# Token routing of a mixture-of-experts kernel: pair weights stored behind the normalized rows, ranks summed by TensorE, lane masks on two engines

## Chip, cores, metric

One core of a Trainium2 chip runs the whole program. The metric is the device time of one execution in microseconds (us), the median over runs.

## The reference, cut to what matters

Eight sequences of 512 tokens (4096 tokens, 256 numbers each) pass through cross attention to a context of 1601 rows, causal self attention, and a mixture of experts. Only the last part is touched by the change:

```python
logits = xf @ w_router                       # 4096 tokens x 8 experts
probs = softmax(logits)
topw, topi = top_k(probs, 2)                 # the two best experts of a token
topw = topw / sum(topw)
combine = sum(one_hot(topi, 8) * topw[..., None])
g, u = silu(xf @ wg[x]), xf @ wu[x]          # hidden size 704
out = sum over experts x of combine[:, x] * ((g * u) @ wd[x])
y = h + out
```

## The kernel before

The kernel is a row of stages with a barrier after each (`Prog.clear`): `prepare_weights`, `project_inputs`, `attention` (cross), `project_self`, `attention` (self), `finish_self`, `route`, `experts`. In a stage each engine has its own written-out program and the engines meet at semaphores: an instruction waits for a count, and a finished one raises one. PE is TensorE, DVE VectorE, ACT ScalarE, POOL GpSimd, SP the queue that issues plain transfers.

**`finish_self`** makes for each batch of 512 tokens the normalized rows, stores them to `hn_rows` in DRAM (a table of 4096 rows of 256 numbers; `store_normed`, L1432), and leaves the router's logits in SBUF. Token number t*128+p lies in partition p, column t (T = 32 columns).

**`route`** sorts the 8192 (token, expert) pairs by expert into tiles of 128 slots. There are 72 tiles, since every expert is padded to a whole tile.
- DVE alone takes the softmax, the two best experts (`first`, `second`, each a 0/1 mask of 128x32x8) and the two pair weights (L1646 to L1680). ACT takes the exponential.
- PE multiplies the choice mask by a triangular matrix (rank of a token within its column, `ps_rank`, L1786) and by ones (count of each column, `ps_total`, L1788). DVE turns the counts of the columns into running sums by five doubling steps (L1684 to L1692).
- DVE counts the tiles of each expert, finds the expert of each tile (`tile_cmp`, `tile_f`, `tile_expert`, L1646 to L1706), then the slot of each pair, and splits it into a tile number and a lane (L1708 to L1723).
- The mask loop has 16 chunks, each of 4 columns of pairs. DVE compares tile numbers to 0..71 (`in_tile`, L1729, 128x4x72) and lanes to 0..127 (`at_lane`, L1733, 128x4x128). POOL multiplies `in_tile` by the token numbers and again by the pair weights (`at_tile`, L1758, two instructions of 128x288). PE sums 4 products of `at_lane` and `at_tile` into `ps_slots` (L1795, 144 columns). The profile lists two instructions for each such f32 product. All masks have two buffers, so chunk n waits for `slots_done` of chunk n-2.
- DVE takes from `ps_slots` three tables in SBUF: token, target row and weight of every slot (L1738 to L1746).
- SP meanwhile loads the down-projection weights of all experts (`wd_sb`, L1772, L1774).

**`experts`** goes over 71 tiles of 128 slots. POOL gathers the rows of a tile from `hn_rows` with an indirect DMA (`gather`, L1888), up to two tiles ahead, and adds the result into `sums` in DRAM with another (`add_up`, L1901). PE turns the rows (L1930), multiplies by gate and up weights (L1941), turns the hidden values (L1949) and multiplies by the down weights (L1959). ACT takes SiLU and scales the result by the slots' weights (`result`, L2009). DVE multiplies gate and up (L2040), copies the turned hidden values (L2046, L2047), and copies one column of the weight table for each tile (`take_weight`, L2034). POOL's own order is: gather of tile k+4, `add_up` of tile k, gather of tile k+5, and so on.

## Time and profile before

| what | value |
|---|---|
| median of 3 runs | 2792.38 us (2789.43 to 2793.11) |
| the profiled execution | 2793.06 us, its span 2791.3 us |
| stages `route` and `experts` by the timeline | about 2117 to 2176 us and from 2177 us on |
| busy share of the span | PE 92%, DVE 64%, ACT 52%, POOL 26% |

The profile lists every instruction of one execution with its engine, line, start and duration. Where an instruction stood idle before it ran, a bracket tells how long and who ended the wait. PEld is the loading of a matmul's stationary operand. PEclk is the granted clock of TensorE as a share of 2.4 GHz, so 0.50 is 1.2 GHz. The chain of work that ended last runs in its last part over the tiles of `experts`.

### The profile page before, as it was taken

The page shows a single profiled execution, that of the slowest core. Times are in us where ns is not written, and L with a number is a line of the kernel's source. Part 1 is how long each engine was busy: PE and PEld are TensorE (multiplying, and loading weights), DVE is VectorE, ACT ScalarE, POOL GpSimd, SP SyncE. Part 2 cuts the span into 40 slices and gives each one's busy share as a digit, 9 for nine tenths or more (in the row PEclk, how much of TensorE's full clock was granted, in tenths as well). Part 3 has the DMA queues.
Part 4 walks back from the last instruction along what each step waited for, and adds up shares of the span by engine and source line. Part 5 has one row for each costly group of instructions (what it writes and reads, how often), then busy time and mean ns, then how long its engine had stood idle before and what let it go on. Part 6 is the DMA issues. An engine that isn't in the chain of part 4 may idle for free. (4 is left out here: it accounts for less than half of the span.)

```text
span 2791.3 us, 47210 instructions
## 1 busy us (share of the span) xinstructions
PE 2575.7 (92%) x14174; PEld 1302.7 (47%) x14175; DVE 1786.7 (64%) x3812; ACT 1453.8 (52%) x2957; POOL 737.0 (26%) x1327
## 2 busy tenths in 40 slices
PE   6999899999999999999997877999884899999996
PEld 4665233333333333333332543444364677777775
DVE  4665888888888888888882766777445222222221
ACT  2333277777777777777775654777521122222221
POOL 4444100000000000000002664666444333333332
PEclk9999699999999999999998998999886999999998
DMA  6777845455555544555513867898574121212123
GB/s 202 224 228 201 117 54 62 57 63 67 67 67 67 62 61 58 61 62 67 67 20 103 244 200 141 162 162 161 135 226 134 25 32 32 32 32 32 32 32 79
DMA packets 494486, 274.38 MB, mean 98 GB/s; under 512 B 309296, under 2 KB 462784, under 8 KB 494112
## 3 DMA queue, kind: packets, MB, share of 16 engines
q1 hardware_dynamic: 472224, 239.77, 44.9%
q0 software_dynamic: 16192, 30.16, 5.7%
q10 hardware_dynamic: 5888, 2.24, 0.4%
q8 instruction: 88, 1.44, 0.3%
q14 instruction: 94, 0.77, 0.1%
HBM read 172.15 MB, written 103.31 MB: 99 GB/s over the span
## 5 line engine op out<-in xcount | busy, mean ns | idle before, releaser
L879 DVE TENSOR_REDUCE att_cross_neg_max<-att_cross_ps_s 128x1 f32<-128x401 f32 x2048 | 1027.2, 567 | 150.8 <-PE att_cross_ps_s L798 148.4
L973 ACT ACTIVATE att_cross_probs<-att_cross_ps_st 128x512 f32<-128x512 f32 (+1 forms) x1664 | 879.4, 601 | 288.9 <-PE att_cross_ps_st L817 276.8
L798 PE MATMUL att_cross_ps_s<-att_cross_k_pack,att_cross_q_pack 96*128 96x401 bf16 x2048 | 655.8, 343 | 11.9 <-DVEq L865 11.4
L817 PE MATMUL att_cross_ps_st<-att_cross_q_pack,att_cross_k_pack 99*128 99x512 bf16 (+1 forms) x1664 | 630.4, 382 | 6.5 <-ACT att_cross_probs L973 5.0
L832 PE MATMUL att_cross_ps_o<-att_cross_probs,att_cross_v_tiles 128*32 128x512 f32 (+1 forms) x3328 | 443.0, 604 | 0.1
L798 PEld LDWEIGHTS att_cross_ps_s<-att_cross_k_pack,att_cross_q_pack 96*128 96x128 bf16 x2048 | 201.1, 98 | 372.2 <-DVE att_cross_neg_max L879 242.9
L921 POOL CAST att_cross_neg_max_parts<-att_cross_neg_max_merged 128x16 bf16<-128x16 f32 x32 | 6.3, 196 | 1134.8 <-DVE att_cross_neg_max_merged L872 1134.8
L817 PEld LDWEIGHTS att_cross_ps_st<-att_cross_q_pack,att_cross_k_pack 99*128 99x128 bf16 (+1 forms) x1664 | 163.8, 99 | 303.5 <-ACT att_cross_probs L973 191.9
L879 DVE TENSOR_REDUCE att_self_neg_max<-att_self_ps_s 128x1 f32<-128x128 f32 (+3 forms) x512 | 221.5, 484 | 96.8 <-PE att_self_ps_s L801 94.7
L973 ACT ACTIVATE att_self_probs<-att_self_ps_st 128x256 f32<-128x256 f32 (+3 forms) x512 | 201.0, 437 | 95.2 <-PE att_self_ps_st L817 86.0
L2046 DVE COPY moe_hiddenT<-moe_ps_h 128x256 f32<-128x256 f32 x142 | 60.2, 424 | 296.9 <-PE moe_ps_h L1949 296.9
L2003 ACT ACTIVATE moe_silu<-moe_ps_g 128x352 f32<-128x352 f32 x142 | 65.7, 463 | 301.3 <-PE moe_ps_u L1941 301.3
L1959 PE MATMUL moe_ps_y<-top_wd_sb,moe_hiddenT 128*128 (+1 forms) x852 | 196.0, 379 | 1.1 <-DVE moe_hiddenT L2047 1.1
L1941 PE MATMUL moe_ps_g<-top_wg_sb,moe_rowsT 128*128 x568 | 192.8, 462 | 0.0
L1941 PE MATMUL moe_ps_u<-top_wu_sb,moe_rowsT 128*128 x568 | 192.3, 461 | 0.0
L798 PE MATMUL att_self_ps_s<-att_self_k_pack,att_self_q_pack 96*128 96x128 bf16 (+3 forms) x512 | 155.3, 313 | 36.1 <-DMA att_self_q_pack<-q_parts 20.2
L1901 POOL DMA_INDIRECT sums<-moe_y,moe_target x71 | 113.4, 1597 | 281.1 <-ACT moe_y L2009 136.2
L1959 PEld LDWEIGHTS moe_ps_y<-top_wd_sb,moe_hiddenT 128*128 128x128 f32 (+1 forms) x852 | 161.6, 190 | 35.1 <-issue 1.4
L934 POOL TENSOR_SCALAR_AFFINE_SELECT att_self_probs<-att_self_probs 128x128 f32<-128x128 f32 x512 | 143.8, 292 | 115.9 <-ACT att_self_probs L973 105.5
L2040 DVE TENSOR_TENSOR moe_hidden<-moe_ps_u,moe_silu 128x352 f32<-128x352 f32 x142 | 73.4, 517 | 133.2 <-ACT moe_silu L2003 131.6
L817 PE MATMUL att_self_ps_st<-att_self_q_pack,att_self_k_pack 99*128 99x256 bf16 (+3 forms) x512 | 151.8, 309 | 2.4 <-ACT att_self_probs L973 1.5
L1941 PEld LDWEIGHTS moe_ps_u<-top_wu_sb,moe_rowsT 128*128 128x128 f32 x568 | 108.5, 191 | 60.7 <-issue 1.0
(220 smaller groups left out, 2886.2 us busy)
## 6 DMA issues: line engine op xcount, KB each, us to landing
att_cross_k_pack<-k_parts SPq DMA_DIRECT2D x192, 200.1 KB, 7.3
k_parts<-in_part SPq DMA_DIRECT2D x72, 256.0 KB, 3.3
in_rows<-in_ctx_dram SPq DMA_DIRECT2D x24, 512.0 KB, 4.5
v_rows<-in_v_biased SPq DMA_DIRECT2D x24, 512.0 KB, 2.9
att_cross_q_pack<-q_parts SPq DMA_DIRECT2D x192, 64.0 KB, 7.8
att_cross_v_tiles<-v_rows SPq DMA_DIRECT2D x128, 96.0 KB
att_self_k_pack<-k_parts SPq DMA_DIRECT2D x192, 64.0 KB, 3.7
att_self_q_pack<-q_parts SPq DMA_DIRECT2D x192, 64.0 KB, 3.7
```

The lines of the kernel that those rows point to most:

```text
L798: mm = nc.tensor.matmul(ps_s[bank][:, 0:w], qp[v.buf][0:SROWS, j, q * P:(q + 1) * P], kp[v.buf][0:SROWS, j, s:s + w], start=True, stop=not ...
L817: mm = nc.tensor.matmul(ps_st[bank_of_step[s]][0:rows, q0:SEQ], kp[u.buf][0:MROWS, j, t * P:t * P + rows], qp[u.buf][0:MROWS, j, q0:SEQ], ...
L832: nc.tensor.matmul(ps_o[j * VW:(j + 1) * VW, q0:SEQ], va[packs.vbuf(u)][0:rows, t, j, :], pr[0:rows, (u.odd * STEPS + t * GH + j) % RING, ...
L879: nc.vector.tensor_reduce(nmax[v.odd][:, j * QT + q, i:i + 1], ps_s[bank][:, 0:w], AX.X, ALU.max, negate=True).then_inc(s_read, 1)
L934: nc.gpsimd.affine_select(out=diagonal, in_=diagonal, pattern=[[1, P]], base=0, channel_multiplier=-1, compare_op=ALU.is_ge, fill=0.0).the ...
L973: nc.scalar.activation(pr[0:rows, (u.odd * STEPS + s) % RING, q0:SEQ], ps_st[bank_of_step[s]][0:rows, q0:SEQ], ACT.Exp).then_inc(exp_done, 1)
L1901: pool.indirect_dma_start(out=sums, in_=y[t.par][:, :], in_offset=None, compute_op=ALU.add, out_offset=bass.IndirectOffsetOnAxis(ap=target ...
L1941: last = nc.tensor.matmul(ps[half][:, 0:HHALF], xT[t.par][:, i, :], wt[:, bass.ds(at, HHALF)], start=(i == 0), stop=(i == KC - 1))
L1959: last = nc.tensor.matmul(ps_y[:, :], hT[half][0:CW[c], c, :], wd[0:CW[c], bass.ds(at, DIM)], start=(half == 0 and c == 0), stop=(half == ...
L2003: nc.scalar.activation(sil[half][:, :], ps_g[half][:, 0:HHALF], ACT.Silu).then_inc(sil_ready, 1)
L2040: nc.vector.tensor_tensor(h[half][:, :], ps_u[half][:, 0:HHALF], sil[half][:, :], ALU.mult)\
L2046: nc.vector.tensor_copy(hT[half][:, 0:CH - 1, :], ps_h[half][:, 0:CH - 1, :])
```

## The change

The weight of a pair is no longer carried through the mask loop. POOL makes a table of 4096 x 8 weights (`dense`, zero for experts not chosen), and ACT's queue stores it into eight more columns of `hn_rows`, whose rows grow from 256 to 264 numbers. The gather brings these with the row. `take_weight` multiplies the tile's eight gathered columns by a one-hot row of the tile's expert (`tile_of_expert`) and adds them up. It now stands first in DVE's step, and POOL's gather waits for it, since it frees the row buffer.

The ranks are summed by PE: the triangular product, then 32 products with ones, each added to all later columns of `ps_rank`, and column T holds the totals. The doubling steps and two additions on DVE fall away.

In the mask loop POOL's `at_tile` is gone. The lane mask is made one column at a time, as a compare with the lane and a multiply by the token number in one instruction of 128x128. In even chunks DVE makes two of them and POOL two, in odd chunks DVE one and POOL three. PE's products have 72 columns instead of 144. The expert of each tile is found after the loop instead of before it.

```diff
@@ finish_self, store_normed
-                    sp.dma_start(batch_rows(hn_rows, b), hn[b % 2][:, :, :]).then_inc(hn_sent[b % 2], 16)
+                    sp.dma_start(batch_rows(hn_rows[:, 0:DIM], b), hn[b % 2][:, :, :]).then_inc(hn_sent[b % 2], 16)
@@ route, new helpers
+        def pool_share(n):
+            return range(2 - n % 2, C)
+        def token_at_lane(engine, n, c):
+            k, t = n * C // T, n * C % T + c
+            return engine.tensor_scalar(at_lane[n % 2][:, c, :], keep["iota_lane"][:, :], lane_of[:, k, t:t + 1],
+                                        keep["token"][:, t:t + 1], ALU.is_equal, ALU.mult)
@@ route, vector
+                nc.vector.memset(chosen[:, T, :], 0.0)
+                nc.vector.memset(past[:, :, 0:1], 1.0)
...
                 dve.wait_ge(ranks_done, 1)
-                nc.vector.tensor_copy(run[0][:, :, :], ps_total[:, :, :])
-                dve.drain()
-                src, step = 0, 1
-                while step < T:
-                    a, b = run[src], run[1 - src]
-                    nc.vector.tensor_copy(b[:, 0:step, :], a[:, 0:step, :])
-                    tt(b[:, step:T, :], a[:, step:T, :], a[:, 0:T - step, :], ALU.add)
-                    src, step = 1 - src, step * 2
-                total = run[src]
...
-                tt(tile_cmp[:, 0:TILES, :], over_e(keep["iota_tile"][:, 0:TILES], TILES),
-                   end[:, :].unsqueeze(1).broadcast_to([P, TILES, E]), ALU.is_ge)
-                reduce(tile_f[:, 0:TILES], tile_cmp[:, 0:TILES, :], ALU.add)
-                nc.vector.tensor_scalar(expert[:, 0:TILES], tile_f[:, 0:TILES], E - 1.0, None, ALU.min)
-                tt(place[:, :, :], total[:, :, :], ps_total[:, :, :], ALU.subtract)
-                tt(place[:, :, :], place[:, :, :], ps_rank[:, :, :], ALU.add)
...
                 for n in range(CHUNKS):
                     if n >= 2:
                         dve.wait_ge(slots_done, n - 1)
-                        dve.wait_ge(tile_ready, n - 1)
                     (in_tile as before)
-                    nc.vector.tensor_tensor(at_lane[n % 2][:, :, :], ...ALU.is_equal).then_inc(lane_ready, 1)
+                    for c in range(pool_share(n)[0]):
+                        last = token_at_lane(nc.vector, n, c)
+                    last.then_inc(lane_ready, 1)
+                tt(past[:, :, 1:E + 1], over_e(keep["iota_tile"][:, 0:TILES], TILES),
+                   end[:, :].unsqueeze(1).broadcast_to([P, TILES, E]), ALU.is_ge)
+                nc.vector.tensor_tensor(of_expert[:, :, :], past[:, :, 0:E], past[:, :, 1:E + 1], ALU.subtract)
+                reduce(tile_f[:, :], past[:, :, 1:E + 1], ALU.add)
+                nc.vector.tensor_scalar(expert[:, 0:TILES], tile_f[:, :], E - 1.0, None, ALU.min)
                 dve.wait_ge(slots_done, CHUNKS)
-                nc.vector.tensor_copy(keep["slot_weight"][:, :], ps_slots[:, 1, :])
@@ route, gpsimd
+                pool.wait_ge(weights_ready, 2)
+                for k, pick in enumerate((first, second)):
+                    nc.gpsimd.tensor_tensor(dense[k][:, :, :], pick[:, :, :], over_e(weights[:, k, :]), ALU.mult)...
+                nc.gpsimd.tensor_tensor(dense[0][:, :, :], dense[0][:, :, :], dense[1][:, :, :], ALU.add)...
+                pool.wait_ge(lanes_ready, 1)
                 for n in range(CHUNKS):
                     if n >= 2:
                         pool.wait_ge(slots_done, n - 1)
-                    pool.wait_ge(in_tile_ready, n + 1)
-                    for a, values in enumerate((keep["token"][:, ts], weights[:, k, ts])):
-                        last = nc.gpsimd.tensor_tensor(at_tile[n % 2][:, :, a, :], in_tile[n % 2][:, :, :], ...)
-                    last.then_inc(tile_ready, 1)
+                    for c in pool_share(n):
+                        last = token_at_lane(nc.gpsimd, n, c)
+                    last.then_inc(pool_lane_ready, 1)
@@ route, sync and scalar
+                sp.wait_ge(dense_sent, 16)
+                act.wait_ge(dense_step, 3)
+                act.dma_start(hn_rows[:, DIM:DIM + E].rearrange("(t p) e -> p t e", p=P), dense[0][:, :, :])
@@ route, tensor
-                nc.tensor.matmul(ps_total..., ones[:, :], chosen...).then_inc(ranks_done, 1)
+                for t in range(T):
+                    last = nc.tensor.matmul(ps_rank[:, t + 1:T + 1, :], ones[:, :],
+                                            chosen[:, t, :].unsqueeze(1).broadcast_to([P, T - t, E]),
+                                            start=False, stop=(t == T - 1))
+                last.then_inc(ranks_done, 1)
...
-                        last = nc.tensor.matmul(ps_slots..., at_lane[n % 2][:, c, :], at_tile[n % 2][:, c, :, :]...)
+                        last = nc.tensor.matmul(ps_slots[:, :], at_lane[n % 2][:, c, :], in_tile[n % 2][:, c, :], ...)
@@ experts, gpsimd, gather
                     pool.wait_ge(turned, t.n + 1)
+                    pool.wait_ge(weight_ready, t.n + 1)
@@ experts, vector
+                dve.sem_inc(weight_ready, 2)
-                def take_weight(t):
-                    dve.wait_ge(y_ready, t.n)
-                    nc.vector.tensor_copy(weight[t.par][:, :], keep["slot_weight"][:, bass.ds(t.n, 1)])...
+                def take_weight(t, first=False):
+                    dve.wait_ge(rows_in[t.par], (t.turn + 1) * 16)
+                    if not first:
+                        dve.wait_ge(y_ready, t.n)
+                    nc.vector.tensor_tensor(weight_if[t.par][:, :], rows[t.par][:, DIM:DIM + EXPERTS],
+                                            keep["tile_of_expert"][:, bass.ds(t.n, 1), :]..., ALU.mult)
+                    dve.drain()
+                    nc.vector.tensor_reduce(weight[t.par][:, :], weight_if[t.par][:, :], AX.X, ALU.add)
                       .then_inc(weight_ready, 1)
@@ experts, vector, step
+                    take_weight(t)
                     turned_hidden(t.next(-1), 1)
-                    take_weight(t)
                     multiply(t, 0)
```

## Rows read from the trace of the kernel before

**Rows 1.** Windows: busy time, counts, granted clock, DMA share of two stretches.
```profile
2138.50:2174.70 36.20, 23.45 (x128) 20.44 (x128) 21.59 (x33) 0.00 (x0) 28.40 (x32) 0.83 0.08 23
...
2181.10:2791.30 610.20, 586.60 (x2556) 434.28 (x2556) 159.71 (x496) 127.14 (x285) 210.32 (x281) 0.98 0.21 37
```

**Rows 2.** Waits from 2117 to 2176 us: total, times, longest.
```profile
PE route_ps_slots L1795 <- POOL route_at_tile L1758: 24.4, 14, 14.3
```

**Rows 3.** Timeline of the ranks and places: start, duration, engine.
```profile
2126.21 0.39 PE L1786 MATMUL route_ps_rank<-route_chosen,top_keep_before_b 128*128 128x256 bf16 x1 [10.11 <-DVE route_chosen L1675]
...
2126.40 0.42 PE L1788 MATMUL route_ps_total<-route_chosen,route_ones 128*128 128x256 bf16 x1
...
2127.28 0.42 DVE L1684 COPY route_run<-route_ps_total 128x256 f32<-128x256 f32 x1
...
2130.49 0.43 DVE L1646 TENSOR_TENSOR route_compare<-route_run,top_keep_constants 128x264 f32<-128x264 f32 x1
...
2132.33 0.76 DVE L1646 TENSOR_TENSOR route_tile_cmp<-top_keep_constants,route_end 128x576 f32<-128x576 f32 x1
...
2134.11 0.41 DVE L1646 TENSOR_TENSOR route_place<-route_run,route_ps_total 128x256 f32<-128x256 f32 x1
```

**Rows 4.** Timeline of the mask loop, its start, one period, its end.
```profile
2138.58 0.46 DVE L1729 TENSOR_TENSOR route_in_tile<-top_keep_constants,route_tile_of 128x288 f32<-128x288 f32 x1
...
2141.15 4.18 PE L1795 MATMUL route_ps_slots<-route_at_tile,route_at_lane 128*128 128x144 f32 x16 [14.34 <-POOL route_at_tile L1758]
...
2154.40 1.22 PE L1795 MATMUL route_ps_slots<-route_at_tile,route_at_lane 128*128 128x144 f32 x8 [1.17 <-POOL route_at_tile L1758]
2155.29 0.66 POOL L1758 TENSOR_TENSOR route_at_tile<-route_in_tile,route_pair_weights 128x288 f32<-128x288 f32 x1
...
2156.18 0.68 DVE L1733 TENSOR_TENSOR route_at_lane<-top_keep_constants,route_lane_of 128x512 f32<-128x512 f32 x1
...
2157.72 1.15 DVE L1733 TENSOR_TENSOR route_at_lane<-top_keep_constants,route_lane_of 128x512 f32<-128x512 f32 x1
...
2158.48 1.22 PE L1795 MATMUL route_ps_slots<-route_at_tile,route_at_lane 128*128 128x144 f32 x8 [1.17 <-POOL route_at_tile L1758]
...
2174.70 0.23 DVE L1738 COPY top_slot_weight<-route_ps_slots 128x72 f32<-128x72 f32 x1 [3.59 <-PE route_ps_slots L1795]
```

**Rows 5.** Timeline of POOL in self attention, four one-input instructions.
```profile
1702.60 1.23 POOL L934 TENSOR_SCALAR_AFFINE_SELECT att_self_probs<-att_self_probs 128x128 f32<-128x128 f32 x4 [0.42 <-ACT att_self_probs L973]
```

**Rows 6.** One line's instructions: DVE with two per-partition scalars.
```profile
L411 DVE TENSOR_SCALAR in_x_normed<-in_rows,in_norm_mean_var,in_norm_std_inv x32: 399/402/2075, 44.7 to 267.5; 128x256 f32<-128x256 f32 x32
```

**Rows 7.** Timeline of PE near the start: 128-column transposes.
```profile
23.43 3.68 PE L362 MATMUL in_ps_t<-top_keep_constants,in_rows 128*128 128x128 f32 x16 [9.16 <-DMA in_rows<-in_ctx_dram]
```

**Rows 8.** Windows: PE busy at either granted clock.
```profile
2147.10:2151.10 4.00, 2.61 (x18) 2.24 (x18) 2.66 (x4) 0.00 (x0) 3.37 (x4) 0.98 0.00 0
...
2106.00:2110.00 4.00, 3.97 (x19) 3.97 (x20) 0.19 (x1) 0.00 (x0) 1.93 (x3) 0.50 0.28 93
```

**Rows 9.** The page's DMA queues: packets, MB, share of 16 engines.
```profile
q10 hardware_dynamic: 5888, 2.24, 0.4%
```

**Rows 10.** Timeline of one expert tile's step.
```profile
2207.77 0.47 ACT L2009 ACTIVATE moe_y<-moe_ps_y,moe_weight 128x256 f32<-128x256 f32 x1 [2.13 <-PE moe_ps_y L1959]
...
2207.90 0.38 PE L1930 MATMUL moe_ps_x<-top_keep_constants,moe_rows 128*128 128x128 f32 x2
...
2208.53 0.28 DVE L2047 COPY moe_hiddenT<-moe_ps_h 96x128 f32<-96x128 f32 x1
...
2209.14 1.59 POOL L1901 DMA_INDIRECT sums<-moe_y,moe_target  x1 [3.99 <-PE moe_ps_x L1930]
...
2211.71 1.02 POOL L1888 DMA_INDIRECT moe_rows<-hn_rows,moe_source  x1 [0.79 <-POOL moe_source L1884]
...
2216.11 0.38 PE L1930 MATMUL moe_ps_x<-top_keep_constants,moe_rows 128*128 128x128 f32 x2
```

**Rows 11.** DMA issues of the experts: count, us to landing.
```profile
moe_rows<-hn_rows,moe_source POOLq DMA_INDIRECT x65, 2.8
```

More of the change, by code:

```diff
@@ L1587, in route @@
     CHUNKS = 2 * T // C
-    logits, expert = keep["logits"], keep["tile_expert"]
+    logits, expert, of_expert = keep["logits"], keep["tile_expert"], keep["tile_of_expert"]
     with ExitStack() as stack:
@@ L1598, in route @@
         top = [p.sb(f"top{i}", [P, T]) for i in range(2)]
-        run = [p.sb(f"run{i}", [P, T, E]) for i in range(2)]
+        weights = p.sb("pair_weights", [P, 2, T])
+        dense = [p.sb(f"dense_weights{i}", [P, T, E]) for i in range(2)]
         place = p.sb("place", [P, T, E])
-        compare = p.sb("compare", [P, E, 64])
+        compare = p.sb("compare", [P, E, T + 1])
         used = p.sb("used_tiles", [P, E])
@@ L1674, in _ @@
                         dve.drain()
-                nc.vector.tensor_tensor(chosen[:, :, :], first[:, :, :], second[:, :, :], ALU.add)\
+                nc.vector.tensor_tensor(chosen[:, 0:T, :], first[:, :, :], second[:, :, :], ALU.add)\
                   .then_inc(chosen_ready, 1)
@@ L1810, in experts @@
         p = Prog(nc, stack, "moe_")
-        rows = [p.sb(f"rows{i}", [P, DIM]) for i in range(2)]
+        rows = [p.sb(f"rows{i}", [P, DIM + EXPERTS]) for i in range(2)]
         xT = [p.sb(f"rowsT{i}", [P, KC, P]) for i in range(2)]
@@ L1819, in experts @@
         weight = [p.sb(f"weight{i}", [P, 1]) for i in range(2)]
+        weight_if = [p.sb(f"weight_if{i}", [P, EXPERTS]) for i in range(2)]
         ps_g = [p.ps(f"ps_g{i}", [P, SEQ]) for i in range(2)]
@@ L2050, in first @@
                 def first(t):
[L2051 removed]
+                    take_weight(t, True)
                     multiply(t, 0)
```

90 lines of the change are left out of this document (45 added, 45 removed).

## The prediction

> **What bounds the kernel now.** I read four views in this order. First the windows by stage. The experts take 610 us, in which PE is busy 587 us at clock 0.98 [rows 1]: PE bounds that stage, and nothing that the change takes from DVE or POOL there can shorten it. The mask loop of the routing takes 36.1 us, and PE works only 23.5 of them, while POOL is busy 28.4 [rows 1]. Second the waits: PE stood 24.4 us in all for POOL's `at_tile` (14.3 of it before the first one) [rows 2]; in the loop POOL is what comes last, chunk after chunk. Third the timeline. Two chunks follow each other every 2158.48 - 2154.40 = 4.08 us [rows 4], 2.04 us a chunk, and the loop ends on PE at 2174.7. Ahead of the loop DVE alone is the chain: from the ranks (2127.28) to the first mask (2138.58) it never waits for another engine [rows 3, 4]. So all that DVE does between the ranks and the first mask, and the loop itself, is on the path that sets the end, since the experts can't start before the barrier. Fourth the step of one expert tile, for slack [rows 10].
>
> **Ahead of the ranks.** Two short fills are added and a drain leaves. A short one-input instruction takes 0.23 us alone [rows 4] (the copy at 2174.70), less in a row. I take +0.1 us.
>
> **The ranks.** Before, two products of 256 bf16 columns start 0.19 us apart [rows 3], the speed of 1.2 GHz, one column a cycle. The new sum has one product of 264 columns and 32 of 256, 248, ... 8 columns. Down to 128 columns these are 17 with 3264 columns together, 2.72 us at 1.2 GHz. The other 15 are shorter than the load of 128 stationary columns, 0.107 us at one column a cycle, 1.6 us. With the first (0.22) and 0.2 for the last one's way through, this is 4.75 us from 2126.3, so 2131.05, and DVE begins its compare at about 2131.15 instead of 2130.49: **+0.7 us**. The doubling steps (3.2 us, 2127.28 to 2130.49) are thus not won but traded for PE's work. If loads don't hide beside products, 17 x 0.107 = 1.8 us come on top. If the clock were high throughout, 2.3 less. While DVE waits, POOL makes `dense`: three two-input instructions of 256 elements. The row of 288 elements takes 0.66 us [rows 4], so 2 us from 2127.0, done before DVE moves again: nothing on the path.
>
> **From the ranks to the first mask.** `tile_cmp`, its reduction and the conversion leave this place: 2134.11 - 2132.33 = 1.78 us [rows 3]. The two additions of 256 elements take 0.41 us and a gap of 0.08 each [rows 3]: 0.98 us. One drain: 0.1. Sum **-2.86 us**. The other instructions keep their shapes, and some read PSUM in place of SBUF (the row of 2134.11 did too, at no higher price). The loop starts at 2138.58 + 0.7 - 2.86 = 2136.4.
>
> **The mask loop.** Three bounds for a chunk.
> - PE: 8 instructions. At 1.2 GHz 16 of them took 4.18 us with 144 columns [rows 4]. With 72 columns the load of 128 stationary f32 columns is longer than the product. The nearest row is 16 transposes of 128 columns in 3.68 us [rows 7], 0.22 each: 1.76 us a chunk, with a gap 1.8. At 2.4 GHz half: 0.9 (8 with 144 columns took 1.22 with their latency [rows 4]).
> - POOL: no row shows a compare-and-multiply on POOL. The nearest has one input and 128x128 elements: four in 1.23 us, 0.31 each [rows 5]. The upper bound is the two-input instruction of 288 elements, 0.66 [rows 4]. Five in two chunks: 1.55 to 3.3 us. I take 0.31 to 0.35, since the shape and the one input agree.
> - DVE: `in_tile` 0.46 [rows 4], and three lane masks in two chunks. With two per-partition scalars and 256 elements DVE took 0.402 us [rows 6]; 128 elements less at 1 ns each (0.68 for 512 against 0.46 for 288 [rows 4]) makes 0.27. Sum 0.92 + 0.81 = 1.73 us in two chunks.
>
> POOL and DVE hinder each other in this trace: the same `at_lane` takes 0.68 us, or 1.15 with POOL at work [rows 4], and the line of [rows 6] has a median of 402 ns and a largest of 2075 ns. So two chunks of masks take between 1.73 (side by side) and 3.28 us (one after the other), with hand-over 1.15 to 1.7 us a chunk. At the high clock a chunk is then 1.35 us, at the low one 1.8 and PE sets it.
>
> The Trainium skill, SBUF — State Buffer, section Who interferes with whom, speaks against a loop split over these two engines: an f32 `tensor_scalar` on DVE can use the pair of ports that GpSimd uses, and whoever is second is blocked entirely. By that rule the loop is 16 x 1.64 + 0.9 = 27.1 us. The trace's 0.68 and 1.15 us [rows 4] agree that one blocks the other, but only in part.
>
> Which clock? The loop starts at 0.50, and in the kernel before it rose about 6 us after PE's start [rows 4, 8] and was 0.83 in the mean of the loop [rows 1]; it stayed 0.50 in a stretch where PE was busy 3.97 of 4 us with products of 8 columns [rows 8]. No row has 72 columns. I take 6 chunks at 1.8 and 10 at 1.35, with 0.9 until the first chunk's masks and 0.1 to DVE: 25.3 us against 36.1: **-10.8 us**. All low gives 29.8 (-6.3), nearly all high and hand-over short 20.5 (-15.6).
>
> **After the loop.** The weight copy leaves: -0.15 us. The search for each tile's expert now stands here: two compares or subtractions of 576 elements, a reduction and a conversion, 1.78 + 0.7 = 2.5 us [rows 3], where 0.76 us, less its fixed part, stands for the added one. It starts when DVE has made its masks of chunk 15, while PE has nearly two chunks ahead (2.7 to 3.6 us, less 0.9 for the masks). About 0.5 us stick out: **+0.35 us** together. Without that cover it would be 2.5.
>
> **The store of the weights.** 4096 pieces of 32 B. The queue that carried small pieces so far has 5888 packets in 0.4% of 16 x 2791 us [rows 9], 30 ns each; 4096 at 30 to 45 ns over 16 engines are 8 to 12 us, from about 2130 to 2142, more beside the wd loads. The stage ends at about 2163, so cover is left unless a piece costs over 130 ns (33 us x 16 / 4096): 0. The normed rows' stores keep their pieces of 1 KB, now 1056 B apart: +0.2 us, bound 0 to 2.
>
> **The experts.** Let S be PE's turn of the next rows, 2207.90 [rows 10]. DVE is free at 2208.81 (S+0.9), the result two tiles back is ready at S+0.34, so `take_weight` is done at S+1.3 and fits before the next hidden copy (DVE is busy 160 of 610 us in this stage [rows 1]). The gather issued then frees one step later than now: index copy and gap 1.0, issue, landing 2.8 us after its start [rows 11], at S+5.2. PE wants these rows at its next turn, 2216.11 or S+8.2 [rows 10]: 3 us are left. `add_up` now stands behind the gather and starts at S+4.5 instead of S+1.24 (2209.14), and it has landed before the `result` that waits for its predecessor. Three instructions in place of one on DVE, 71 times, lie under PE. I take +0.3 us for the first tiles.
>
> **The sum.** +0.1 +0.7 -2.86 -10.8 +0.35 +0.2 +0.3 = -12.0 us against the profiled 2793.06, so 2781.0. The median lies 0.7 us under it: **2780.5 us**.
>
> **Rivals.**
> - *A, POOL's compare-and-multiply is dear.* At 0.66 us two chunks take 3.3 + 0.5 = 3.8 us, the loop 31.3, and the time is 2786.5. At 0.82 (4.6 us for two) nothing is left of the gain of the whole change. For it: no row of this operation, two scalars are read besides. Against: [rows 5]. Chance 0.12.
> - *B, the gather's new wait takes the place of the weight table.* If rows land later than S+8.2, every tile is longer by the lateness, 70 us for each us. This ends on the slower side, from 3 us more than counted on. For it: the gather moves one whole step, and POOL has two indirect transfers in line behind it. Against: the slack in [rows 10, 11]. At 1 us of lateness 2850. Chance 0.06.
> - *C, the scattered store ends last*, from 130 ns a piece; at 170 ns the stage ends 10 us later, which makes 2791: no change. Chance 0.05.
>
> The Trainium skill, DMA: Bandwidth & Descriptors, section Specifications, says that pieces under 512 B are read, modified and written, which would speak for C. No row here shows a 32 B store; [rows 9] show small pieces without such a price.
>
> - *D, ports serialize wholly*, as the rule above has it: 2782.3, within the forecast.
>
> **The numbers.** The forecast has 0.74 with D, A 0.12, B 0.06, C 0.05, and something unseen 0.03. About 0.2% (5.6 us) is what a measurement of this kernel can tell from no change. The forecast's cases reach from 2775 (high clock, short hand-over) to 2785.5 (clock low throughout, ranks unhidden). With A's upper row the range is 2774 to 2787. Faster 0.82 (forecast and part of A), same 0.10 (the dearer end of A, and C), slower 0.08.
>
> **What would show it.** Compare starts near 2131 and the first mask near 2136.5; 16 chunks from there to `slots_done` in 20 to 30 us; PE's wait names DVE and POOL less, and its clock in that window tells which case it is; POOL's 128x128 mask at about 0.3 us; experts at 8.21 us a tile, with PE busy throughout; `ps_x` waiting for `moe_rows` would be B, SP waiting long after the last slot would be C.

## Result, and the profile after

| | before | after |
|---|---|---|
| median, runs on the same chip | 2792.23 us (20 runs) | 2795.92 us (20 runs) |
| ratio, 95% interval | | 1.0013 [1.0007, 1.0019] |
| the profiled execution, its span | 2793.06, 2791.3 | 2794.20, 2792.5 |

The change makes the kernel a little slower, by 0.13%. The interval does not reach 1, but the size is below the 0.2% that the prediction took for the least it could tell apart. 12 us were forecast to be won, and the median lies above the forecast's range of 2774 to 2787.

The timelines of the two executions, cut at the same events, show where. "First fill" is DVE's memset of `ones` at the start of `route`; "first mask" is the first `in_tile`; the loop ends where DVE reads `ps_slots`.

| stretch | before | after | difference | forecast |
|---|---|---|---|---|
| first fill to `compare` | 13.38 | 13.08 | -0.30 | +0.8 |
| `compare` to first mask | 8.09 | 5.17 | -2.92 | -2.86 |
| mask loop | 36.12 | 42.26 | **+6.14** | **-10.8** |
| loop's end to first gather | 3.58 | 3.47 | -0.11 | +0.35 |
| first gather to first `ps_x` | 2.88 | 3.46 | +0.58 | 0 |
| first `ps_x` to the end | 610.14 | 610.47 | +0.33 | +0.3 |
| sum | 674.2 | 677.9 | +3.7 | -12.2 |

The sum of +3.7 us is close to what the medians show (2795.92 - 2792.23). The profiled spans differ by 1.2 only, because the stages ahead of `route` were 2.5 us shorter in this one execution; over the runs below the first fill comes between 2111.7 and 2121.1 us, whatever the edit. The forecast column lacks the +0.2 us of the normed rows' stores, which lie ahead of the first fill. One row is far off, the mask loop. Here is the timeline of the changed kernel (start, duration, engine, line, names; in brackets the idle time before and who ended it), which answers to [rows 3, 4]:

```profile
2123.69 0.40 PE L1793 MATMUL route_ps_rank<-route_chosen,top_keep_before_b 128*128 128x264 bf16 x1 [10.10 <-DVE route_chosen L1688]
...
2123.89 3.74 PE L1796 MATMUL route_ps_rank<-route_chosen,route_ones 128*128 128x256 bf16 x32
...
2126.66 0.45 ACTq L1787 DMA_DIRECT2D hn_rows<-route_dense_weights  x1
...
2127.67 0.43 DVE L1657 TENSOR_TENSOR route_compare<-route_ps_rank,top_keep_constants 128x264 f32<-128x264 f32 x1 [3.14 <-PE route_ps_rank L1796]
...
2132.84 0.49 DVE L1724 TENSOR_TENSOR route_in_tile<-top_keep_constants,route_tile_of 128x288 f32<-128x288 f32 x1
...
2135.13 1.96 PE L1805 MATMUL route_ps_slots<-route_in_tile,route_at_lane 128*128 128x72 f32 x8 [7.50 <-POOL route_at_lane L1650]
...
2147.66 3.66 PE L1805 MATMUL route_ps_slots<-route_in_tile,route_at_lane 128*128 128x72 f32 x16 [1.40 <-POOL route_at_lane L1650]
2149.65 0.46 DVE L1724 TENSOR_TENSOR route_in_tile<-top_keep_constants,route_tile_of 128x288 f32<-128x288 f32 x1 [2.38 <-PE route_ps_slots L1805]
2149.72 4.41 POOL L1650 TENSOR_SCALAR route_at_lane<-top_keep_constants,route_lane_of 128x128 f32<-128x128 f32 x5 [0.65 <-PE route_ps_slots L1805]
...
2152.72 3.66 PE L1805 MATMUL route_ps_slots<-route_in_tile,route_at_lane 128*128 128x72 f32 x16 [1.40 <-POOL route_at_lane L1650]
...
2170.53 0.84 DVE L1657 TENSOR_TENSOR route_past_expert<-top_keep_constants,route_end 128x576 f32<-128x576 f32 x1
...
2173.03 0.20 DVE L1735 TENSOR_SCALAR top_tile_expert<-route_tile_f 128x72 int32<-128x72 f32 x1
...
2173.11 1.96 PE L1805 MATMUL route_ps_slots<-route_in_tile,route_at_lane 128*128 128x72 f32 x8 [1.54 <-POOL route_at_lane L1650]
2175.10 0.23 DVE L1738 TENSOR_SCALAR route_token_f<-route_ps_slots 128x72 f32<-128x72 f32 x1 [1.87 <-PE route_ps_slots L1805]
```

The period of two chunks is 2152.72 - 2147.66 = 5.06 us, before it was 4.08 [rows 4]. Read one period as a circle. POOL starts at 2149.72 with three masks for an odd chunk, each of them a row of the timeline here:

```profile
2149.72 1.15 POOL L1650 TENSOR_SCALAR route_at_lane<-top_keep_constants,route_lane_of 128x128 f32<-128x128 f32 x1 [0.65 <-PE route_ps_slots L1805]
...
2150.86 0.79 POOL L1650 TENSOR_SCALAR route_at_lane<-top_keep_constants,route_lane_of 128x128 f32<-128x128 f32 x1
...
2151.63 0.94 POOL L1650 TENSOR_SCALAR route_at_lane<-top_keep_constants,route_lane_of 128x128 f32<-128x128 f32 x1
```

They end at 2152.57, 2.85 us after the start. PE waits for the third of them (1.40 us idle) and starts 0.15 later, at 2152.72. After another 2.06 us POOL begins again, at 2154.78: a chunk of PE's takes 1.96 when it stands alone (the row of 2173.11), and 0.10 go to the hand-over. 2.85 + 0.15 + 2.06 = 5.06. The two masks of the even chunk lie beside PE's work. So three things stand on this circle: POOL's own price of a mask (0.79), PE's chunk at the low clock, and 0.5 us by which the first and the third mask are longer than the second. The first starts 0.07 us behind DVE's `in_tile` (2149.65), the third while the next `in_tile` is under way; e5 below shows whose doing that is. The instructions of the masks' line (shortest, median and longest, ns):

```profile
L1650 POOL TENSOR_SCALAR route_at_lane<-top_keep_constants,route_lane_of x40: 789/799/1152, 2132.8 to 2172.0; 128x128 f32<-128x128 f32 x40
L1650 DVE TENSOR_SCALAR route_at_lane<-top_keep_constants,route_lane_of x24: 334/341/428, 2133.3 to 2170.3; 128x128 f32<-128x128 f32 x24
```

The waits from 2117 to 2176 us (total, times, longest), which answer to [rows 2]:

```profile
DVE route_in_tile L1724 <- PE route_ps_slots L1805: 24.3, 14, 2.7
PE route_ps_slots L1805 <- POOL route_at_lane L1650: 17.8, 9, 7.5
```

A mask costs POOL 799 ns in the median; DVE makes the same one in 341. Five take POOL 4.41 us, 0.88 each, of which 0.5 us in all are those longer ones. PE's wait for POOL has not gone: it was 24.4 us before with a first wait of 14.3 [rows 2], and is 17.8 now with a first one of 7.5, so some 10 us behind the first chunk in either kernel, and PE is slower meanwhile. The windows (busy time and count of PE, PEld, DVE, ACT and POOL, granted clock, DMA share, GB/s), which answer to [rows 1, 8]:

```profile
2132.84:2175.10 42.26, 29.63 (x128) 28.06 (x128) 15.92 (x44) 0.00 (x0) 35.81 (x40) 0.50 0.16 50
2147.10:2151.10 4.00, 3.44 (x16) 3.47 (x16) 0.89 (x3) 0.00 (x0) 3.35 (x5) 0.50 0.00 0
2179.00:2789.00 610.00, 586.86 (x2556) 434.45 (x2556) 175.42 (x568) 127.00 (x285) 212.60 (x283) 0.98 0.22 38
```

The clock is 0.50 from the first mask to the end of the loop. Before it was 0.83 in the mean [rows 1] and 0.98 in the same window [rows 8]. The experts are as before: 587 us of PE in 610, clock 0.98.

### The profile page after: what moved, and what is told of

It reads as the page before. It is cut to its first block and busy times, and to the rows that moved or that the text cites. A ratio compares the mean times of both kernels' runs of the same rounds, so it can differ in the third digit from the quotient of the medians.

```text
span 2792.5 us, 47629 instructions
## 1 busy us (share of the span) xinstructions
PE 2582.0 (92%) x14205; PEld 1313.0 (47%) x14206; DVE 1792.0 (64%) x3880; ACT 1454.0 (52%) x2957; POOL 748.8 (27%) x1338
## 5 line engine op out<-in xcount | busy, mean ns | idle before, releaser
L832 PEld LDWEIGHTS att_cross_ps_o<-att_cross_probs,att_cross_v_tiles 128*32 128x32 f32 (+1 forms) x3328 | 65.6, 108 | 151.5 <-ACT att_cross_probs L973 128.9
```

The source lines that it names most:

```text
L832: nc.tensor.matmul(ps_o[j * VW:(j + 1) * VW, q0:SEQ], va[packs.vbuf(u)][0:rows, t, j, :], pr[0:rows, (u.odd * STEPS + t * GH + j) % RING, ...
```

## Experiments

Each is an edit of the changed kernel unless it says otherwise. "Loop" is the stretch of the table above in the run's one profile. Ratios are to the kernel before, run on the same chip beside it.

**e1: all masks on DVE.** This takes POOL out of the loop and leaves all the rest.

```diff
 def pool_share(n):
-    return range(2 - n % 2, C)
+    return range(C, C)
...
-                    for c in range(pool_share(n)[0]):
+                    for c in range(C):
```

POOL's loop over the chunks and PE's wait for it are taken out too.

> The changed kernel with all 64 lane masks on DVE and POOL idle in the mask loop. Theory 1 (POOL's mask instruction of about 0.88 us, five in two chunks, is what made the loop 42.3 us): DVE needs 0.46 + 4 x 0.29 = 1.6 us a chunk and PE at 1.2 GHz 1.83, so a chunk is 1.9 us, the loop about 31 us and the kernel 11 us faster than the changed one, about 2785 (8 us or 0.3% under the kernel before). Rival 2 (TensorE's low clock with 72 columns is the bound, POOL only seems to be late): a chunk stays near 2.5 us, the loop above 38 us and the time at 2792 or more. PE's granted clock should stay 0.50 by both.

Measured: 2783.14 us (10 runs), ratio 0.9972 [0.9962, 0.9982], loop 30.92 us. So POOL's part in the masks costs 42.26 - 30.92 = 11.3 us of loop. A short and a long window of this run, columns as above:

```profile
2140.00:2144.00 4.00, 4.00 (x20) 3.86 (x19) 3.35 (x13) 0.00 (x0) 0.00 (x0) 0.50 0.22 76
...
2136.00:2160.00 24.00, 24.00 (x109) 23.19 (x108) 19.36 (x67) 0.00 (x0) 0.00 (x0) 0.50 0.18 55
```

Its group of products from 2142 to 2158 us (count, busy us, mean ns, idle):

```profile
L1797 PE MATMUL route_ps_slots<-route_in_tile,route_at_lane 128*128 128x72 f32 x72 | 16.6, 424 | 0.0
```

PE is busy 24.00 of 24 us and the clock stays at 0.50. PE is the bound here, at 1.2 GHz, with 1.8 us a chunk.

**e6: the same with 144 columns.** PE reads `in_tile` twice, and the second half of the sum is thrown away. This is more work for PE, at the column count of the kernel before.

```diff
-    last = nc.tensor.matmul(ps_slots[:, :], at_lane[n % 2][:, c, :], in_tile[n % 2][:, c, :],
+    last = nc.tensor.matmul(ps_slots[:, :, :], at_lane[n % 2][:, c, :],
+                            in_tile[n % 2][:, c, :].unsqueeze(1).broadcast_to([P, 2, TILES]),
...
```

> As the run with all masks on DVE, but the products have 144 columns again (each tile mask read twice). If the number of columns is what let TensorE's clock rise to 2.4 GHz in the kernel before, the clock rises some 6 us after the loop's start, PE then needs 1.2 us a chunk, DVE's 1.6 us (with hand-over 1.8) sets the pace and the loop is 3 x 2.0 + 13 x 1.8 = 29 to 30 us: 1 to 2 us less than with 72 columns. If the clock depends on something else it stays at 1.2 GHz, a chunk is 2.0 us and the loop 33 us: 2 us more than with 72 columns.

Measured: 2779.28 us (6 runs), ratio 0.9954 [0.9939, 0.9969], loop 27.02 us. Twice the columns make the loop 3.9 us shorter, more than the 1 to 2 us expected. The intervals of e1 and e6 overlap, but of the ten times of e1 only one lies below the longest of e6. Two windows of this run:

```profile
2140.00:2144.00 4.00, 3.46 (x22) 3.21 (x21) 3.56 (x14) 0.00 (x0) 0.00 (x0) 0.82 0.57 184
2144.00:2148.00 4.00, 3.37 (x24) 2.82 (x24) 3.99 (x15) 0.00 (x0) 0.00 (x0) 1.00 0.00 0
```

Its groups of products and of masks from 2142 to 2158 us:

```profile
L1797 PE MATMUL route_ps_slots<-route_in_tile,route_at_lane 128*128 128x144 f32 x88 | 13.6, 295 | 2.8 <-DVE route_at_lane L1650 2.8
L1650 DVE TENSOR_SCALAR route_at_lane<-top_keep_constants,route_lane_of 128x128 f32<-128x128 f32 x46 | 12.8, 343 | 0.0
```

The clock rises in the first of these windows and is 1.00 from the second on. A product takes 295 ns on average instead of 424, and DVE, busy 3.99 of 4 us with masks of 0.34, is the bound.

**e5: all masks on POOL.** DVE keeps only `in_tile`, whose two-input instructions leave it idle for most of the loop.

```diff
 def pool_share(n):
-    return range(2 - n % 2, C)
+    return range(0, C)
```

DVE's masks and PE's wait for them are taken out too.

> POOL makes all 64 lane masks, DVE only the tile masks, so that DVE is idle most of the loop and has no one-input instruction in it. If the price on POOL is its own, the median stays 0.80 us and a chunk takes 4 x 0.88 + 0.4 = 3.9 us, the loop 63 us, the time about 2813 to 2817. If DVE's tensor_scalar blocked POOL, the median falls towards 0.35 and the loop is 30 to 35 us.

Measured, one run: 2810.75 us against 2791.71, loop 54.99 us, where 63 were expected. Its groups from 2140 to 2176 us:

```profile
L1650 POOL TENSOR_SCALAR route_at_lane<-top_keep_constants,route_lane_of 128x128 f32<-128x128 f32 x46 | 37.4, 826 | 0.0
...
L1724 DVE TENSOR_TENSOR route_in_tile<-top_keep_constants,route_tile_of 128x288 f32<-128x288 f32 x11 | 5.0, 459 | 32.6 <-PE route_ps_slots L1801 32.6
```

And two rows of its timeline, the only instruction of DVE's in this chunk and the mask of POOL's that starts beside it:

```profile
2143.00 0.46 DVE L1724 TENSOR_TENSOR route_in_tile<-top_keep_constants,route_tile_of 128x288 f32<-128x288 f32 x1 [4.55 <-PE route_ps_slots L1801]
...
2143.18 0.94 POOL L1650 TENSOR_SCALAR route_at_lane<-top_keep_constants,route_lane_of 128x128 f32<-128x128 f32 x1
```

POOL works without a pause, 826 ns a mask in this window (median of the loop 790), while DVE is idle 32.6 us. With no mask of DVE's beside it the price stays at 790: that part is POOL's own, and neither DVE's masks nor two engines blocking each other make it. The longer masks stay too, one in each chunk, the one that starts inside `in_tile`. So what holds POOL up is DVE's two-input `in_tile`, not DVE's masks. Undisturbed, five masks would take 5 x 0.78 = 3.9 us from start to start (an estimate from these rows) instead of 4.41. A chunk is 3.26 us here: three masks at 0.78 and one at 0.93.

**e3b: what of the instruction is dear.** The kernel of e1, and in it POOL, idle otherwise, makes four of each of five kinds of 128x128 instruction into tables that nobody reads.

```diff
+for i in range(4):
+    nc.gpsimd.tensor_scalar(spare[0][:, i, :], iota, lane, tok, ALU.is_equal, ALU.mult)
+    nc.gpsimd.tensor_scalar(spare[1][:, i, :], iota, lane, None, ALU.is_equal)
+    nc.gpsimd.tensor_scalar(spare[2][:, i, :], iota, 5.0, 3.0, ALU.is_equal, ALU.mult)
+    nc.gpsimd.tensor_copy(spare[3][:, i, :], iota)
+    nc.gpsimd.tensor_tensor(spare[4][:, i, :], iota, lane.broadcast_to([P, P]), ALU.mult)
```

> All lane masks on DVE, 72 columns. POOL runs beside the loop, waited for by nobody before the stage's end, four rounds of five kinds of instruction on 128x128 f32: (1) compare with a per-partition scalar and multiply by another, (2) compare with a per-partition scalar only, (3) compare and multiply with constants, (4) a copy, (5) a two-input multiply. Their results are not used. Theory 1a (the two per-partition scalars are dear): (1) 0.80, (2) 0.55, (3) 0.30, (4) 0.30. Theory 1b (compare with multiply is dear as such): (1) and (3) 0.80, (2) 0.5 or less. Theory 1c (this kind of instruction has a high fixed price on POOL): (1), (2), (3) all about 0.80, (4) 0.30. (5) by the rows of 16, 130 and 256 elements is about 0.45.

Measured, one run: 2783.84 us, loop 31.35 us. POOL's groups (names: both = compare and multiply by per-partition scalars):

```profile
L1761 POOL TENSOR_SCALAR route_spare_both_<-top_keep_constants,route_lane_of 128x128 f32<-128x128 f32 x4 | 3.8, 952 | 6.1 <-DVE route_lane_of L1718 6.1
L1763 POOL TENSOR_SCALAR route_spare_constants_<-top_keep_constants 128x128 f32<-128x128 f32 x4 | 2.7, 678 | 0.3
L1762 POOL TENSOR_SCALAR route_spare_compare_<-top_keep_constants,route_lane_of 128x128 f32<-128x128 f32 x4 | 2.6, 652 | 0.0
L1765 POOL TENSOR_TENSOR route_spare_two_input_<-top_keep_constants,route_lane_of 128x128 f32<-128x128 f32 x4 | 1.8, 448 | 0.0
L1764 POOL COPY route_spare_copy_<-top_keep_constants 128x128 f32<-128x128 f32 x4 | 1.3, 332 | 0.2
```

These means hold instructions that DVE's `in_tile` held up: of the four of the first kind two start within 0.07 us of an `in_tile`'s start and take 1.09 and 1.07 us, one takes 0.86, and one 0.79, as in the changed kernel. The usual row of each kind is: copy 0.29 to 0.37 us, two-input multiply 0.40, compare with one scalar 0.65, compare and multiply with constants 0.65, with two scalars 0.79. A compare costs twice the copy, with constants for operands too, and the form with two scalars read from SBUF costs 0.14 more. None of the three theories had these numbers; the nearest is 1c, that the kind of instruction is dear. The affine-select of [rows 5] is priced like the copy. The number of inputs says nothing of the price. (An earlier form, e3, with a two-input compare as the fifth kind, gave no time.)

**e2 and e10: POOL makes one mask of four, with 72 columns (e2) and with 144 (e10, with the edit of e6 besides).**

```diff
 def pool_share(n):
-    return range(2 - n % 2, C)
+    return range(C - 1, C)
```

> The changed kernel with one lane mask of every chunk on POOL and three on DVE, 72 columns. If PE at 1.2 GHz (1.83 us a chunk with PE busy 4.00 of 4 us when DVE made all masks) is the bound once POOL is off the path, this brings nothing more: DVE 1.35 us, POOL 0.88, PE 1.83, loop 30.5 to 31.5 us and 2783 to 2784, the same as with all masks on DVE. If the masks' making had been the bound, the loop would fall to 24 us and the time to 2777.

> The same split (one mask on POOL, three on DVE) with products of 144 columns, so that TensorE's clock rises as it did with all masks on DVE (loop 27.0 us, DVE the bound at 1.6 us a chunk). If the pieces are independent: the masks take DVE 0.46 + 3 x 0.29 = 1.35 us a chunk, PE 1.2: 3 chunks at 2.0 and 13 at 1.4, loop 24.5 us, time about 2777. If DVE's and POOL's instructions block each other (theory of the shared port), the sum of both counts, 1.35 + 0.8 = 2.15 us a chunk, and the loop is 34 us, slower than with all masks on DVE.

Measured: e2 2782.85 us (6 runs), ratio 0.9967 [0.9952, 0.9981], loop 29.12 (expected 30.5 to 31.5), PE busy 4.00 of 4 us at clock 0.50, with 1.71 us a chunk. e10 2777.92 us (5 runs), ratio 0.9955 [0.9942, 0.9969], loop 25.08 (expected 24.5). The pair repeats what e1 and e6 showed, 4.0 us of loop for the columns alone, though the intervals of the two whole times overlap. Two windows of e10:

```profile
2140.00:2144.00 4.00, 3.95 (x20) 3.76 (x20) 3.02 (x10) 0.00 (x0) 2.66 (x3) 0.64 0.60 192
2144.00:2148.00 4.00, 3.62 (x26) 3.06 (x25) 3.91 (x14) 0.00 (x0) 3.52 (x4) 1.00 0.00 0
```

The groups of its masks from 2142 to 2158 us:

```profile
L1650 POOL TENSOR_SCALAR route_at_lane<-top_keep_constants,route_lane_of 128x128 f32<-128x128 f32 x12 | 13.8, 1150 | 2.8 <-PE route_ps_slots L1805 2.2
...
L1650 DVE TENSOR_SCALAR route_at_lane<-top_keep_constants,route_lane_of 128x128 f32<-128x128 f32 x36 | 11.0, 364 | 0.0
```

Here a mask costs POOL 1150 ns and DVE 364. In this window every mask of POOL's starts some 0.07 us behind an `in_tile`, as the first of five does in the changed kernel, and that one took 1.15 too, with one mask of DVE's beside it instead of three. One of four on POOL wins 1.9 us of loop over none (25.08 against 27.02), which the intervals of the whole time don't separate.

**e11: 144 columns with the split of the change.** The edit is that of e6; POOL keeps its five masks of eight.

> The changed kernel with one edit: TensorE's products in the mask loop read in_tile twice and have 144 columns instead of 72 (the second half is thrown away). The split of the masks stays: five of eight on POOL. Theory (POOL's price first, the clock second): five masks at 0.88 us start to start are 4.4 us for two chunks, and the kernel as changed takes 5.06 because POOL also waits some 0.65 us for TensorE at 1.2 GHz. If the clock rises, PE gives the buffers back sooner, and the pair takes 4.4 to 4.7 us: loop 36 to 38.5 us instead of 42.3, time 2790 to 2792.5, that is level with the kernel before. Rival 1 (the price alone): the loop stays at 42 us and the time at 2795, whatever the clock. Rival 2 (the clock is the main cause and POOL's price follows from the stretch in which both work): the loop comes down to 27 to 30 us as in the runs with 144 columns and few POOL masks, time near 2782. Rival 3: with POOL setting the pace, PE is too idle for the clock to rise even with 144 columns; it stays 0.50 and the loop gets longer, 43 to 45 us.

Measured: 2790.54 us (11 runs), ratio 0.9994 [0.9984, 1.0003], loop 39.36 us. So 144 columns alone bring the changed kernel level with the kernel before, as the theory had it; its loop was expected at 36 to 38.5 and is 0.9 longer. Rival 1 is out since the loop is 2.9 us shorter, rival 2 since it is far from 27 to 30, rival 3 since the clock rises. Four windows of its loop:

```profile
2140.00:2144.00 4.00, 2.44 (x16) 2.06 (x16) 1.74 (x5) 0.00 (x0) 4.00 (x5) 1.00 0.00 0
...
2148.00:2152.00 4.00, 3.46 (x16) 3.49 (x16) 0.84 (x3) 0.00 (x0) 3.32 (x5) 0.60 0.00 0
2152.00:2156.00 4.00, 2.27 (x14) 1.80 (x14) 1.69 (x5) 0.00 (x0) 4.00 (x5) 0.93 0.00 0
2156.00:2160.00 4.00, 3.36 (x14) 3.04 (x14) 1.03 (x3) 0.00 (x0) 3.45 (x5) 0.50 0.00 0
```

And one row of its timeline:

```profile
2150.63 8.82 POOL L1650 TENSOR_SCALAR route_at_lane<-top_keep_constants,route_lane_of 128x128 f32<-128x128 f32 x10 [0.68 <-PE route_ps_slots L1805]
```

At clock 1.00 POOL runs ten masks with no pause, 0.88 each, and PE is idle 1.56 of 4 us. Then the clock falls to 0.50 to 0.60 for some windows and rises again, so part of POOL's wait of 0.65 us in two chunks comes back.

**e7: the ranks alone.** The kernel before, with PE's 32 products with ones in place of the doubling steps.

```diff
-    nc.vector.tensor_copy(run[0][:, :, :], ps_total[:, :, :])
...
+    for t in range(T):
+        last = nc.tensor.matmul(ps_rank[:, t + 1:T + 1, :], ones[:, :],
+                                chosen[:, t, :].unsqueeze(1).broadcast_to([P, T - t, E]),
+                                start=False, stop=(t == T - 1))
```

> The kernel before with one part of the change alone: ranks summed by PE, doubling steps and two additions on DVE gone; expert search, mask loop, weight table and gather as before. Theory: the compare starts 0.3 us earlier than before (PE's 32 products took 3.74 us in the changed kernel), the two additions (0.98) leave, first mask 1.3 to 1.4 us earlier, everything behind it unchanged: 2790.5, no more than 0.05% faster and not to be told from no change. Rival: TensorE is left in another state of its clock by the 4 us of products, so that the mask loop starts at 2.4 GHz and is 3 to 4 us shorter: 2787.

Measured: 2792.52 us (12 runs), ratio 0.9998 [0.9988, 1.0008]. The first mask comes 1.0 us earlier after the first fill (20.46 against 21.47 us). 1.3 were expected; the missing 0.3 went ahead of the ranks, where the edit changes next to nothing (9.38 us from the fill to PE's first product, 9.10 in the kernel before). But the loop of the profile is 38.24 us. Its window has

```profile
2141.51:2179.75 38.24, 26.85 (x128) 24.79 (x128) 21.32 (x33) 0.00 (x0) 27.40 (x32) 0.74 0.12 35
```

a clock of 0.74 where the kernel before had 0.83 [rows 1], with the same work in it. Why the clock was lower in this execution was not tried. It is the slowest of the twelve (2798.69 us, 6.2 above their median), so its loop is no measure of the edit, and one profile can't tell chance from cause.

**e9: the weight path with the loop of before.** The weights come with the rows and PE sums the ranks, as changed; the mask loop is that of the kernel before less one of its multiplies: one `at_lane` of 128x512 on DVE, one multiply of `in_tile` by the token numbers on POOL, 144 columns.

```diff
-                    for c in range(pool_share(n)[0]):
-                        last = token_at_lane(nc.vector, n, c)
+                    nc.vector.tensor_tensor(at_lane[n % 2][:, :, :],
...
-                    for c in pool_share(n):
-                        last = token_at_lane(nc.gpsimd, n, c)
+                    nc.gpsimd.tensor_tensor(at_tile[n % 2][:, :, :], in_tile[n % 2][:, :, :],
+                                            keep["token"][:, ts].unsqueeze(2).broadcast_to([P, C, TILES]),
```

> The changed kernel's ranks and weight path with the mask loop of the kernel before, only without the second multiply on POOL: lane mask one compare of 128x512 on DVE, tile mask multiplied by the token numbers on POOL (one instruction of 128x288), products of 144 columns as before. In the kernel before POOL set the pace with 0.98 + 0.66 us a chunk and waits. Theory: with one instruction POOL needs 1.0 us, DVE 0.46 + 0.69 to 1.15, PE 1.2 at 2.4 GHz, so 1.4 to 1.6 us a chunk, loop 25 to 27 us, time 2777 to 2779. It tells what the weight path alone gives when nothing dear replaces it. If blocking between the two engines' two-input instructions decides, a chunk stays near 1.9 us, loop 31 us, 2783.

Measured: 2778.82 us (5 runs), ratio 0.9954 [0.9942, 0.9967], loop 27.75 us (expected 25 to 27), clock 0.82 from 2140 to 2144 us and 1.00 after it. The group of POOL's instructions from 2142 to 2158:

```profile
L1765 POOL TENSOR_TENSOR route_at_tile<-route_in_tile,top_keep_constants 128x288 f32<-128x288 f32 x11 | 10.5, 956 | 6.3 <-DVE route_in_tile L1726 6.3
```

With one POOL instruction of 956 ns a chunk the loop is 8.4 us shorter than before (36.12): the second multiply, and the wait for it, was what the old loop's pace came from.

**e8: bf16 masks.** A token number t*128+p is split into p and t, which ACT and POOL multiply into `in_tile`, so that PE's products are bf16, one instruction each. `at_lane` is one DVE instruction a chunk.

```diff
+                    nc.gpsimd.tensor_tensor(at_tile[n % 2][:, 1, :, :], in_tile[n % 2][:, :, :],
+                                            keep["iota_tile"][:, ts].unsqueeze(2).broadcast_to([P, C, TILES]),
...
+                    nc.scalar.activation(at_tile[n % 2][:, 0, :, :], in_tile[n % 2][:, :, :], ACT.Copy,
+                                         scale=keep["token"][:, 0:1]).then_inc(low_ready, 1)
```

> The changed kernel's ranks and weight path, with another mask loop: the lane mask is one two-input compare of 128x512 on DVE with a bf16 result, the tile mask is multiplied by the token's low part on ACT (one per-partition scalar, 128x288) and by its high part on POOL (two-input multiply, 128x288), both with bf16 results, and PE makes one bf16 product of 144 columns a column in place of f32 ones (the profile lists two instructions for an f32 product, one for a bf16 one). DVE 0.46 + 0.68 to 1.15, POOL 0.66 to 1.0, ACT about 0.45, PE 0.5 at 1.2 GHz. If the engines' own prices decide: 1.3 to 1.6 us a chunk, loop 22 to 26 us, time 2774 to 2778. If hand-over between four engines decides (POOL and ACT start only after the tile mask, PE after both): 0.46 + 1.0 + 0.5 + 0.4 = 2.4 us in two buffers is still under 2 x 1.5, so no more than that.

Measured: 2777.75 us (5 runs), ratio 0.9955 [0.9941, 0.9968], loop 25.49 us. PE is busy 1.9 of 4 us and the clock stays 0.50; DVE is the bound, for its instruction beside POOL's multiply takes

```profile
L1729 DVE TENSOR_TENSOR route_in_tile<-top_keep_constants,route_tile_of 128x288 f32<-128x288 f32 x10 | 9.2, 916 | 0.0
```

916 ns instead of the 0.46 of [rows 4]. Most of them start some 0.4 us after a multiply of POOL's. ACT works beside them too, but the kernel before, where ACT is idle, has an `in_tile` of 0.92 us as well (2139.56), with POOL's multiplies under way.

## Why the prediction was wrong

**The step that failed: the size of POOL's mask in the mask loop's term.** The prediction took 0.31 to 0.35 us from the affine-select of [rows 5], "since the shape and the one input agree", and held 0.66 [rows 4] for the upper bound. Measured are 0.79 undisturbed, and 0.88 from start to start with what `in_tile` adds: some two and a half times the value taken, and above the bound too. Shape and number of inputs were the wrong likeness, what counts is the kind of operation (e3b). Five masks in two chunks take POOL 4.41 us, more than the 4.08 of the kernel before, and on the circle of one buffer three of them stand in line with PE's chunk. This was rival A, with its point of decision (0.82 us leaves nothing of the gain), at a chance of 0.12. It should have had far more, as no row showed the operation and only an equal shape spoke against it. Removing POOL from the loop gives 11.3 us back, leaving it one of four 13.1. This step alone carries the time out of the range: e1 and e2 keep the low clock and lie at 2783, inside it, while e11 has the high clock for part of the loop and lies at 2790.5, outside.

**The second step: the clock with 72 columns.** The prediction let it rise after six chunks, from what 144 columns do [rows 4, 8]. It never rose: not in the changed kernel, nor in e1 and e2, where PE was busy 4.00 of 4 us throughout. Adding 72 useless columns makes it rise and wins 3.9 and 4.0 us of loop where PE is the bound, and 2.9 where POOL is (e6, e10, e11). The price of a chunk at the low clock was right: 1.71 to 1.83 us measured, 1.8 forecast. With the clock low and POOL cheap the prediction had 29.8 us for the loop, and e1 and e2 have 30.9 and 29.1. That e10's loop, at 25.08 us, meets the 25.3 of the forecast is a coincidence: it has another split and 144 columns. Four versions beat the kernel before by 0.45%: e6, e8, e9 and e10, 2777.8 to 2779.3 us, with intervals that overlap. What it is in the 72-column stream that holds the clock down was not tried apart and stays open. e8 keeps the low clock too, with 144 columns of bf16 and PE busy at most 1.9 of 4 us.

**Point by point, the rest.**
- The ranks: -0.3 instead of +0.7. PE's 32 products took 3.74 us, not 4.5. The 17 long ones took the 2.72 forecast. The 15 short ones took 1.02 with the last one's way through, not 1.8: their starts lie 0.10 and at the end 0.03 us apart, so the load of 0.107 forecast for each did not set their pace. DVE waited 3.14 us for them. The doubling steps are traded for PE's work, as forecast, with a small gain.
- `compare` to first mask: -2.92 against -2.86, right to the instruction.
- The expert search after the loop: done at 2173.2, ahead of PE's last chunk, which ends at 2175.07. It sticks out by nothing, where 0.5 us were forecast, since PE's last chunk still waits 1.54 us for POOL's masks.
- The 32-byte store, rival C: the queue went from 5888 packets [rows 9] to

```profile
q10 hardware_dynamic: 10000, 2.37, 0.5%
```

and the store issued at 2126.66 landed 6.3 us later, at most 6.3 x 16 / 4112 = 25 ns a piece, beside the loads of `wd_sb`. The read-modify-write that the Trainium skill, DMA: Bandwidth & Descriptors, section Specifications, names for such pieces left no mark that this stage could feel.
- The gather's new wait, rival B: the step of one tile, which answers to [rows 10],

```profile
2208.44 0.38 PE L1941 MATMUL moe_ps_x<-top_keep_constants,moe_rows 128*128 128x128 f32 x2
...
2209.07 0.28 DVE L2065 COPY moe_hiddenT<-moe_ps_h 96x128 f32<-96x128 f32 x1
2209.51 0.17 DVE L2048 TENSOR_TENSOR moe_weight_if<-moe_rows,top_tile_of_expert 128x8 f32<-128x8 f32 x1 [0.17 <-issue]
...
2209.76 0.16 DVE L2052 TENSOR_REDUCE moe_weight<-moe_weight_if 128x1 f32<-128x8 f32 x1
...
2210.18 0.18 POOL L1895 COPY moe_source<-top_slot_token 128x1 int32 x1 [3.96 <-DVE moe_weight L2052]
...
2211.18 1.03 POOL L1899 DMA_INDIRECT moe_rows<-hn_rows,moe_source  x1 [0.82 <-POOL moe_source L1895]
```

has `take_weight` done at S+1.5 (S = 2208.44, PE's turn) and the gather issued at S+2.7. With 2.8 us to landing, the median as in [rows 11] though rows now stand 1056 B apart, they are in place at S+5.5 (forecast S+5.2), 2.7 us before PE's turn at S+8.2. POOL waits here for DVE and nobody waits for POOL. The tile stays at 8.2 us, and the stage at 610.
- Rival D, ports that serialize wholly: not for the two engines' masks. In the changed kernel DVE's mask takes 341 ns and POOL's 799, and with no mask on DVE (e5) POOL's median is 790. The Trainium skill, SBUF — State Buffer, section Who interferes with whom, has the second of the two blocked entirely. For DVE's masks the traces don't bear that out. For the two-input `in_tile` they come near it: a mask of POOL's that starts with 0.39 us of it to run is 0.36 longer, one that starts with 0.27 to run (e5) 0.15 longer. Thus 0.5 us of each 5.06 are such a wait, a small part of the miss.
- The first gather to `ps_x` took 0.58 us longer. It lies between 2.86 and 3.48 in the profiles of all runs: e1 and e6, which gather the same wider rows, have 2.89 and 2.86, and e7, with the old rows, has 3.48. So the wider rows don't cost it; what does was not looked for.

## What to carry to other kernels

Price an instruction on an engine by a row of the same operation on that engine; an equal shape and an equal number of inputs are no substitute, and where no such row exists the case "it is two or three times dearer" deserves a large chance. When work is dealt out between two engines, write down the circle that one buffer runs through (fill, read, give back) with both prices, not only the sum of each engine, and look which instruction of the one engine starts just behind which of the other. Before a product of PE is made narrower, ask whether it is the length of the product or the load that sets the pace, and whether the clock will still rise.

## What the runs showed of the hardware

- TensorE stayed at 1.2 GHz (clock 0.50) for the 24 us from 2136 to 2160 in e1, with PE busy 24.00 and PEld 23.19 of them, on f32 products of 72 columns behind loads of 128. The same products with 144 columns went to 2.4 GHz (e6). The Trainium skill, TensorE: Matmul & The Clock Gate, section HAM oscillation — how this bites in real kernels, puts a low clock down to gaps in which PE is idle; in these 24 us there was no gap, so the busy share of the profile didn't tell whether the clock would rise.
- POOL's prices for 128x128 f32, where no `in_tile` starts with them: copy 0.29 to 0.37 us, two-input multiply 0.40, compare with one scalar 0.65 (e3b), compare and multiply with two 0.79 (e3b, e5); DVE makes the last in 0.34. The Trainium skill, GPSIMD Engine Reference, section 4.1 Engine selection, calls one-input work on this engine roughly as fast as on VectorE. The copy fits that roughly (DVE's copy of this shape took 0.23 us in the kernel before, at 2129.99), the compare does not.
- Contention depends on the kind and on who starts first. DVE's compare of 288 elements with two inputs takes 0.46 us alone and 916 ns when POOL's two-input multiply has begun 0.4 us earlier (e8). A mask of POOL's that begins 0.07 us after that compare takes 1.15 us instead of 0.79, in the changed kernel as in e10, while the compare keeps its 0.46. The two engines' masks hardly touch each other: DVE's go from 341 to 364 ns (e10).
